# ScalarE order in the last stage: the activations of chunk 13 move ahead of the root of chunk 12's last norm

## The reference

```python
x = x + layernorm(attention(layernorm(x)))        # 16 heads of 16, causal
h = layernorm(x)
_, idx = top_k(h[:, 0, :] @ Wr + br, 2)           # two of eight experts for each batch
h1 = gelu(einsum('bsd,bkde->bkse', h, W1[idx]) + b1[idx])      # exact gelu
o  = einsum('bkse,bkef->bksf', h1, W2[idx]) + b2[idx]
x = x + layernorm(sum(o, axis=1) / 2)
```

## Time and profile before

| what | us |
|---|---|
| median of 3 runs | 1973.89 |
| lowest and highest | 1973.69 and 1978.52 |
| the profiled execution, its own time | 1975.9 |
| its span, first to last instruction | 1974.2 |
| TensorE busy in it | 1939.4 |
| VectorE busy in it | 1783.2 |
| ScalarE busy in it | 1363.5 |

### The profile page before, as it was taken

The page is one execution under the profiler, slowest core; times in us unless marked ns, Lnnn a source line. Parts: engine busy times, 40 slices in busy tenths (PEclk is TensorE's granted clock), DMA queues, the critical chain, the costliest instruction groups (busy, mean ns, idle before and its releaser), DMA issues. The chain is left out here.

```text
span 1974.2 us, 39435 instructions
## 1 busy us (share of the span) xinstructions
PE 1939.4 (98%) x15684; PEld 850.2 (43%) x15684; DVE 1783.2 (90%) x3574; ACT 1363.5 (69%) x1655; POOL 294.5 (15%) x358
## 2 busy tenths in 40 slices
PE   9999999999999999999999999999999998999998
PEld 6655333333333333333333333333333342667665
DVE  7877899999999999999999999999998985799984
ACT  5766777777777777777777777777777768333432
POOL 4332201111111101011111101010111111322000
PEclk9999999999999999999999999999999999999999
DMA  6876615040414324050503233040506213344321
GB/s 178 252 231 202 146 47 97 7 94 11 90 34 75 58 43 94 9 93 7 94 25 82 41 62 78 22 94 9 93 18 148 61 50 114 87 127 124 94 68 43
DMA packets 151706, 162.93 MB, mean 83 GB/s; under 512 B 58466, under 2 KB 124386, under 8 KB 151522
## 3 DMA queue, kind: packets, MB, share of 16 engines
q1 hardware_dynamic: 146658, 151.98, 32.5%
q0 software_dynamic: 4864, 8.44, 2.0%
HBM read 100.03 MB, written 60.29 MB: 81 GB/s over the span
## 5 line engine op out<-in xcount | busy, mean ns | idle before, releaser
L627 DVE TENSOR_REDUCE b_pmax<-b_ring 128x1 f32<-128x512 f32 (+3 forms) x2264 | 1318.2, 647 | 51.6 <-PE b_ring L617 38.7
L1341 ACT ACTIVATE b_prob<-b_psS 128x1024 f32<-128x1024 f32 (+3 forms) x1280 | 1084.5, 895 | 341.2 <-PE b_psS L1384 337.4
L1384 PE MATMUL b_psS<-g_qT,g_kT 64*128 64x512 bf16 (+7 forms) x5120 | 811.3, 347 | 11.3 <-ACT b_prob L1341 5.5
L617 PE MATMUL b_ring<-g_kT,g_qT 64*128 64x512 bf16 (+3 forms) x2478 | 706.6, 347 | 0.1
L1401 PE MATMUL b_psO<-b_prob,g_v 128*32 128x512 f32 (+3 forms) x5120 | 597.0, 541 | 0.3 <-POOL b_prob L1311 0.3
L1384 PEld LDWEIGHTS b_psS<-g_qT,g_kT 64*128 64x128 bf16 (+1 forms) x5120 | 291.9, 94 | 321.1 <-ACT b_prob L1341 177.9
L617 PEld LDWEIGHTS b_ring<-g_kT,g_qT 64*128 64x128 bf16 x2478 | 221.8, 94 | 384.0 <-DVE b_pmax L627 317.4
L1311 POOL TENSOR_SCALAR_AFFINE_SELECT b_prob<-b_prob 128x512 f32<-128x512 f32 x256 | 162.4, 634 | 1275.0 <-ACT b_prob L1341 1274.9
L615 PE MATMUL b_ring<-later,query_of 64*128 64x128 bf16 x982 | 186.5, 219 | 0.8 <-ACT a_v L1097 0.5
L1401 PEld LDWEIGHTS b_psO<-b_prob,g_v 128*32 128x32 f32 x5120 | 102.9, 108 | 168.5 <-issue 133.2
L1755 PE MATMUL c_psH<-c_yT,c_w1e 128*128 128x512 f32 x256 | 118.3, 611 | 10.0 <-ACT c_hT L1676 7.0
(11 more groups left out here) (162 smaller groups left out, 1060.3 us busy)
## 6 DMA issues: line engine op xcount, KB each, us to landing
qk_parts<-a_parts SPq DMA_DIRECT2D x64, 384.0 KB, 4.5
g_qT<-qk_parts SPq DMA_DIRECT2D x184, 128.0 KB, 4.3
g_kT<-qk_parts SPq DMA_DIRECT2D x184, 128.0 KB, 5.5
out_sums<-b_outT SPq DMA_DIRECT2D x64, 256.0 KB, 2.8
v_ones<-a_v SPq DMA_DIRECT2D x16, 544.0 KB, 6.0
g_v<-v_ones SPq DMA_DIRECT2D x32, 272.0 KB, 5.4
a_x<-in_L_attn_x SPq DMA_DIRECT2D x16, 512.0 KB, 5.3
c_x<-in_L_attn_x SPq DMA_DIRECT2D x15, 512.0 KB, 4.9
```

Of the source, the lines that this page charges most:

```text
L617: ins_ = self.nc.tensor.matmul(to, groups.qT[own, g, h // 2, 0, t * P:(t + 1) * P], groups.kT[own, g, h // 2, 0, pc * CH:pc * CH + w], sta ...
L627: self.nc.vector.tensor_reduce(pmax[:, c % 2].rearrange("p (h t) n -> p h t n", t=TT)[:, heads[0]:heads[-1] + 1:2, qt, pc], bank[:, 0:k * ...
L1341: nc.scalar.activation(prob[:, j % PBUF, 2 * s:2 * s + 2, off:CH], psS[:, 2 * s:2 * s + 2, off:CH], ACT.Exp).then_inc(exp_done, 1)
L1384: ins_ = nc.tensor.matmul(psS[:, 2 * s + p, off:CH], kT[own, g, s, ab, kt * P:(kt + 1) * P], qT[own, g, s, ab, c * CH + off:(c + 1) * CH], ...
```

## The change

`UNLED` goes from 14 to 13. It is read in two places only, both in the loop of ScalarE quoted above.

```diff
         LAST = B * NC - 1
 
-        UNLED = LAST - 1
+        UNLED = LAST - 2
         PARTS = [slice(0, TT // 2), slice(TT // 2, TT)]
```

## The result

| | before | after |
|---|---|---|
| median of 20 runs, us | 1974.84 | 1971.87 |
| lowest and highest, us | 1971.09 and 1980.52 | 1966.23 and 1976.16 |
| span of the profiled execution, us | 1974.2 | 1974.5 |

The ratio is 0.9982, with a 95% interval of 0.9974 to 0.9989. That is 3.6 us less, between 2.2 and 5.1, and within the 0.3% for which the prediction gave 0.89. The forecast was 1969.3 and the range 1967 to 1973.

A forecast was written before the change was run, and what follows sets the result against it. Near the end TensorE's chain was taken to bound the kernel. A gain of 4.82 us less 0.2 for the late turn gave 4.6, so 1973.89 became 1969.3 us, range 1967 to 1973.

The forecast's parts named there:

- The wait: In `hidden(13)`, TensorE's ninth matmul waits for ScalarE, starting at 1923.92 instead of 1920.90; removing this gains 3.02 us.
- The clock's part: Second half of `hidden(13)` takes 5.24 us instead of 3.43 at the lowered clock; without the wait, 1.81 us is gained.
- The late turn of chunk 15: `turn_y(15)` on TensorE waits for `c_y`, behind chunk 12's later root: between 0 and 0.25 us lost, taken as 0.2.
- Both claims that the first activation costs nothing: First gelus of chunks 13 and 14 on ScalarE, behind a copy and table load, don't stop TensorE: 0 us each.
- the cover: ScalarE's 0.42 us idle ahead of chunk 14's second product; gone when the copy comes some 0.1 us later.
- the clock's rival: In `hidden(13)`, the clock's part isn't there or falls elsewhere: gain 2.8 us, time 1971.1; chance 0.22.
- That nothing is seen: Other executions are bound elsewhere in the tail, or the runs scatter over the gain: 1973.9; chance 0.08.
- That each switch holds more than its row: Each ScalarE table switch costs more than shown, say 1.3 us more: 1.1 us of gain remains, 1972.8; chance 0.08.
- The slower rival: The turn of chunk 15 takes the old wait's place on TensorE: a loss of 2.0 us, 1975.9; chance 0.03.

The follow-up runs named there:

- the filler: Kernel before plus three unused products on TensorE between the second and third product of `hidden(13)`; `hidden(13)` 9.99 us, ratio to before 0.9985 (0.9974 to 0.9997).
- the pads: Changed kernel plus two unread ScalarE copies, behind `copy_y(14)` and ahead of chunk 12's root; `hidden(13)` 7.31 us, from its start to the end 52.9 us; not timed.
- the later comparison: Changed kernel, no further edit, timed against the kernel before in five rounds on one chip: ratio 0.9976 (0.9962 to 0.9990).

## Why the prediction was right

**The mechanism** was right at each step: the wait of `hidden(13)` and the fall of the clock behind it are both gone, and nothing but a tenth of a microsecond took their place. **The sum** was 4.82 - 0.2 = 4.6 us, and the last stretch is 4.7 us shorter in the profiles.

**The terms.** The wait, 3.02 us, is confirmed by the filler, which leaves it untouched. The clock's part was put at 1.81 us and is 1.70; the other 0.11 is the restart, seen behind the waits of 0.17, 0.27 and 0.40 us too. Their sum, 4.82, is what the change removed. The late turn of chunk 15 was taken at 0.2 and costs 0.10, since most of the 0.28 us by which the weight loads are late doesn't reach the matmuls. Both claims that the first activation costs nothing held. The prediction put the cover, at 0.42 us of idle time, at some 0.1 us; with the same idle time in chunk 13 the pads give 0.17, and the restart's 0.1 comes on top of a delay beyond it.

**The time** came out at 1971.87, 2.6 us above the forecast. Of this 1.0 is the base: the median of before was 1973.89 over three runs, from which the forecast was worked out, and 1974.84 over twenty. The other 1.6 is that the medians are 3.0 us apart and not 4.6. The ratio gives 3.6, the later comparison 4.7, and the intervals of both hold 4.6. The scatter ahead of the change, with profiled spans from 1966.6 to 1974.5 us for one kernel, is large enough for that. That the later ratio has just 4.7 us at its centre is luck: its interval runs from 2.0 to 7.5 us. No term of the sum is off by more than some 0.1 us.

**The rivals.** By its time alone the clock's rival (1971.1) would have looked like the truth, and both intervals hold its 2.8 us too; three profiles of before, each with the clock down behind the wait, and the filler speak against it. That nothing is seen is excluded by the ratio, whose interval ends at 0.9989. That each switch holds more than its row would have left 1.1 us and is excluded by the last stretch. The rule of the Trainium skill, ScalarE: Activation LUTs, section "Table sets: the hidden batching unit", to batch activation calls by set, speaks against this edit: it adds two switches. The trace shows 1.28 us of load for each and no draining. The one ahead of chunk 14's first gelu is covered; the one ahead of the root of chunk 12 delays the root, and the late turn costs 0.10 us. The slower rival's mechanism is real: the pads make the turn late one for one, and with the edit moved one step back a late root holds up VectorE, the copy behind it and so TensorE, and the gain is lost.

## What to carry to other kernels

A step may be moved ahead of another on an in-order engine if the engine behind the one put off has slack just there: the same line, one chunk earlier, where VectorE had no gap, gave all of the gain back. Ask of each added instruction how thick its cover is: here the first activation had 0.17 us to spare, and the root had none. When the whole time scatters by more than the edit is worth, measure from a mark just before the edit to the end: that stretch repeated within 0.1 us while the spans differed by 7.

## What the runs showed that wasn't expected

A wait of TensorE can cost more than its length. Behind 3.0 us of waiting came 1.7 us of slow clock in each of three profiles, and behind 3.9 us the same 5.23 us for the next eight matmuls. Behind waits of 0.4 and 1.2 us came none. The wait of 2.6 or 2.7 us at the head of the stage lies between: the clock fell within or right behind it in eight of 13 profiles and stayed at 1.00 in five, and that made up to 3 us of difference. Three products that nobody needs, six matmul records put into the wait of 3.0 us, gave the 1.7 us back in both profiles of that kernel. The Trainium skill, TensorE: Matmul & The Clock Gate, section "What's actually happening", has the clock follow how busy the engine has been, and the filler agrees. It also has the number of slow matmuls vary from run to run: at the wait of 3.0 us no profile shows that, at the wait ahead of the stage's first `hidden` they do.
